# A tuned fp32 early-fusion layer on one core: scores and two second-layer passes of each expert-loop iteration issued earlier

## The reference

```python
z = jnp.einsum('nd,sdr->nsr', xf, P)              # 8 groups of R=16
scores = jnp.einsum('nsr,smr->nsm', z, C)         # 64 experts per group
topv, topi = jax.lax.top_k(scores, K)             # K = 4
w = jax.nn.softmax(topv, axis=-1)
h = jax.nn.gelu(jnp.einsum('nsr,nskrh->nskh', z, W1g) + b1g)   # first layer, 32 hidden
yl = jnp.einsum('nskh,nskhr->nskr', h, W2g) + b2g              # second layer
comb = jnp.einsum('nskr,nsk->nsr', yl, w)
out = jax.nn.gelu(comb @ G1 + g1b) @ G2 + g2b
```

## Time and profile before

| | us |
|---|---|
| median of 3 executions (954.18 to 957.66) | 955.19 |
| the profiled execution, its own time | 961.78 |
| its span, first to last instruction | 960.0 |
| PE busy / ACT busy / DVE busy / POOL busy in the span | 882.4 / 592.4 / 669.0 / 477.4 |
| mean granted TensorE clock, share of full speed | 0.965 |

### The profile page before, as it was taken

How to read it: one execution, slowest core, us unless ns; L and a number is a source line. 1 busy time by engine, 2 the same in 40 slices (tenths; PEclk the granted TensorE clock), 3 DMA queues, 4 the chain that set the end, 5 groups by cost and what they waited for, 6 DMA issues and landing times.

```text
span 960.0 us, 16073 instructions
## 1 busy us (share of the span) xinstructions
PE 882.4 (92%) x5394; PEld 397.4 (41%) x5394; DVE 669.0 (70%) x1670; ACT 592.4 (62%) x869; POOL 477.4 (50%) x446
## 2 busy tenths in 40 slices
PE   2599999999999977798989999999899989999997
PEld 1257777767877765322222222222222222222222
DVE  4355555566677468587778787788878877877774
ACT  0221211125322344599988897889988898988784
POOL 0043434233254435476766565656666665665453
PEclk8699999999999987799999998999999999999999
DMA  9500001000000166676879787878787978798772
GB/s 263 195 1 1 1 1 71 1 2 1 2 1 6 23 99 109 190 211 225 237 239 255 229 256 215 251 232 251 239 253 232 256 230 267 238 255 284 246 256 99
DMA packets 89053, 154.14 MB, mean 161 GB/s; under 512 B 30100, under 2 KB 55957, under 8 KB 88322
## 3 DMA queue, kind: packets, MB, share of 16 engines
q1 hardware_dynamic: 87998, 149.86, 51.5%
q10 hardware_dynamic: 972, 3.24, 2.4%
HBM read 138.81 MB, written 15.83 MB: 161 GB/s over the span
## 4 chain that ended last, share of the span: by engine, by line
PE 71%; DVE 11%; ACT 10%; issue 4%; DMA 1%; SPq 1%; POOL 1%; ACTq 1%; DVEq 0%; POOLq 0%
PE ps L764 15%; PE ps L701 14%; PE ps L424 8%; PE ps L432 5%; PE ps L740 4%; PE ps L491 4%; PE ps L483 3%; DVE ring L1495 3%; DVE ring L1498 3%; PE ps L500 3%; PE ps L541 2%; PE ps L461 2%; PE ps L513 2%; ACT ring L1058 2%; ACT L943 1%
## 5 line engine op out<-in xcount | busy, mean ns | idle before, releaser
L1697 POOL TENSOR_TENSOR ring<-ring,wbc 128x512 f32<-128x512 f32 x192 | 244.6, 1279 | 157.6 <-ACT ring L1065 149.0
L1495 DVE TENSOR_TENSOR ring<-ps,ring 128x1024 f32<-128x1024 f32 x192 | 234.7, 1223 | 95.8 <-ACT ring L1058 50.1
L701 PE MATMUL ps<-zst,w1st 99*128 99x512 bf16 x768 | 219.4, 390 | 22.5 <-ACT ring L1058 15.0
L764 PE MATMUL ps<-ring,w2cur 128*32 128x512 f32 x1536 | 205.8, 609 | 0.0
L1058 ACT ACTIVATE ring<-ps 128x1024 f32<-128x1024 f32 x192 | 197.3, 1027 | 6.3 <-PE ps L701 6.1
L1552 POOL TENSOR_TENSOR t<-t 128x768 f32<-128x768 f32 x48 | 87.4, 1832 | 206.2 <-DVE t L1186 206.2
L1067 ACT ACTIVATE ps<-ps 128x512 f32<-128x512 f32 x192 | 114.3, 595 | 46.2 <-PE ps L701 46.1
L1498 DVE TENSOR_TENSOR ring<-ps,wbc 128x512 f32<-128x512 f32 x192 | 131.1, 683 | 1.2 <-DMA wbc<-w_rows 1.2
L701 PEld LDWEIGHTS ps<-zst,w1st 99*128 99x128 bf16 x768 | 60.1, 98 | 162.6 <-issue 37.4
L1184 DVE TENSOR_TENSOR t<-ps,rope 128x768 f32<-128x768 f32 x48 | 45.8, 953 | 110.6 <-PE ps L432 74.4
L1065 ACT ACTIVATE ring<-ps 128x512 f32<-128x512 f32 x192 | 115.7, 603 | 0.4 <-PE ps L701 0.4
(11 more groups left out here) (165 smaller groups left out, 1147.3 us busy)
## 6 DMA issues: line engine op xcount, KB each, us to landing
wbc<-w_rows SPq DMA_DIRECT2D x192, 512.0 KB, 5.2
w2cur<-in_w SPq DMA_DIRECT2D x48, 256.0 KB, 4.9
w_parts<-wp SPq DMA_DIRECT2D x72, 64.0 KB, 3.2
zst<-z_parts SPq DMA_DIRECT2D x72, 64.0 KB, 5.2
w1st<-w_parts ACTq DMA_DIRECT2D x12, 256.0 KB
wst<-w_parts SPq DMA_DIRECT2D x24, 128.0 KB, 4.6
z_parts<-zp SPq DMA_DIRECT2D x6, 384.0 KB, 5.5
wst<-w_parts SPq DMA_DIRECT2D x24, 96.0 KB, 4.8
```

The costliest lines, as they stand in the source:

```text
L701: return pe.matmul(bank(to), w1st[0:99, 4 * a + j, col:col + P], zst[0:99, (i // 2) % 2, j, :], start=True, stop=True)
L764: mm = pe.matmul(bank(YBANK, 0, 512, 32 * j, 32 * j + 32), w2cur[:, n, j, :], ring[:, (4 * g + j) % RING, :], start=False, stop=(n == 7 an ...
L1495: dve.tensor_tensor(v, ps[:, WBANK * 512:WBANK * 512 + 1024], v, ALU.mult).then_inc(s["duo_done"], 1)
L1697: pool.tensor_tensor(ring[:, slot, :], ring[:, slot, :], wbc[:, g % 4, 1, :], ALU.mult).then_inc(s["tri_done"], 1)
```

## The change

The scores of tile `i + 6` are issued at the end of group n = 3, behind `two_first` of the next group, and not at the start of n = 4; between the two places PE had nothing else. In iterations 5, 9, 13 and 17 (`finals`) they keep their old place. Directly behind, PE issues `second(8i+2)` and `second(8i+3)`, which used to stand inside the bodies of n = 4 and n = 5; those bodies now have none. On ACT `copy_scores` moves, except in the `finals` iterations, from the end of n = 4 to the end of n = 3, directly behind `exps`. For iterations 1 to 3 the wait for `z_e` moves with the scores.

```diff
+        def finals(i):
+
+            return i % 4 == 1 and i > 1
...
-                    if n == 4:
-                        pe.wait_ge(s["z_e"], i + 3)
-                if n == 4 and tile + 1 < TILES:
+                if n == 4 and tile + 1 < TILES and finals(i):
                     pe.wait_ge(s["wT_done"], tile)
-                    if i > 4:
-                        pe.wait_ge(s["fin_h"], 2 * ((i - 1) // 4))
+                    pe.wait_ge(s["fin_h"], 2 * ((i - 1) // 4))
                     scores(tile + 1, PBANK)
                 if g + 1 < GROUPS:
                     duo_firsts(g + 1)
                     tri_first(g + 1)
-                if g >= 2 and g % 16 != 2:
+                if g >= 2 and g % 16 != 2 and not (tile < TILES and n in (4, 5)):
                     second(g - 2)
...
                 if g % 16 == 2:
                     second(g - 2)
+                if n == 3 and tile < TILES:
+                    if tile + 1 < TILES and not finals(i):
+                        pe.wait_ge(s["wT_done"], tile)
+                        if i in (1, 2, 3):
+                            pe.wait_ge(s["z_e"], i + 3)
+                        scores(tile + 1, PBANK)
+                    second(g - 1)
+                    second(g)
...
-                if n == 4 and tile + 1 < TILES:
+                if n == (4 if finals(i) else 3) and tile + 1 < TILES:
                     copy_scores(tile + 1, PBANK)
```

## The result

The changed kernel takes **990.06 us** in the median of four executions (981.35 to 998.12), beside 956.42 for the kernel before. Two of the four (996.34 and 998.12 us, with the lowest mean granted clocks) lie more than 1.5% above the fastest and are left out of the ratio, which is **1.0254 (95% interval 1.0218 to 1.0289)**. A later measurement with six executions gives 985.16 us (979.76 to 995.65) and 1.0257 (1.0225 to 1.0288).

The account below looks back on a forecast made before the run. Two chains were taken to bound the kernel: PE's row of work, and ACT from the exponentials to n = 7. Terms 1.99 + 0.78 + 12.74 - 0.2 = +15.3 us on the 955.2 median gave 970.5 us, range 961 to 982.

Parts of the forecast that it names:

- PE has time to spare in the odd iterations only, none in the even ones: PE busy 22.15 of 22.25 us in iteration 10, 19.73 of 22.20 in 11, with a 1.83 us gap before n = 4.
- The passes are ready and cost no wait: Behind the scores, the two moved second passes find products and weights ready; two take 2.0 us.
- The table load does not run ahead of the waiting copy: On in-order ACT, load and GELU follow the waiting copy; first GELU of n = 4 at scores' start + 2.97 us.
- Net +1.82 us in an ordinary even iteration: Iteration 10: first GELU of n = 4 3.04 us later, less 1.22 back by n = 6, passed fully into the time.
- -0.03 us in an odd one: Odd iterations without finals: first GELU of n = 4 1.19 us later, less 1.22 back; taken as 0.
- Finals 0: Iterations 5, 9, 13 and 17: net 0 to -0.4 us each, taken as 0 because PE waits for DVE anyway.
- The sum: Iterations 0 and 2 +1.99 and +0.78, seven even ones +12.74, iteration 18 -0.2: +15.3 us.
- Rival 3: TensorE's clock falls where PE is thin between scores and n = 7: two to four more falls, 977 to 983 us; chance 0.15.
- the mechanism: ACT's wait for the scores in the even iterations passes through into the time: 963 to 976 us, chance 0.67.
- Rivals 1 and 2: 1: PE's filled gaps are gained, 942.6 us, chance 0.08; 2: ACT's delay is absorbed, 953 to 958 us, chance 0.10.

Follow-up runs that it names:

- third experiment: The change in the odd iterations only (finals included), even ones exactly as in the kernel before: 958.76 us, ratio 1.0012 against the kernel before.
- kernel with fillers: The changed kernel plus five filler matmuls, results unused, in PE's idle time per iteration with moved scores: 972.11 us, ratio 1.0140 against the kernel before.
- second experiment: The changed kernel with the second passes back in n = 4 and 5, scores and copy as changed: 1014.74 us, ratio 1.0593 against the kernel before.

## Why the prediction was right in its cause and short in size

- **PE has time to spare in the odd iterations only, none in the even ones.** Right. It decides the case, and the third experiment shows it.
- **The passes are ready and cost no wait.** Right: 1.92 us for both, directly behind the scores.
- **The table load does not run ahead of the waiting copy; the first GELU starts at the scores' start + 2.97 us.** Right: 668.11 - 665.15 = 2.96. No drain showed beside the load either (copy's end to load 0.02, load to GELU 1.29), so the row was rightly taken over the 1380 ns that the Trainium skill gives for a drain (ScalarE: Activation LUTs, What ACT_TABLE_LOAD costs).
- **Net +1.82 us in an ordinary even iteration.** Right: +1.80. Its parts hold too: in iteration 10 the delay is 3.02 us at the first GELU of n = 4, 2.54 at that of n = 5, where the copy is gone, and 1.79 at the copy of the gates, whose transposes are in time. Iteration 14 gains only +1.27 (24.05 with fillers, 22.78 before), because it had been longer before; the prediction counted it like the others.
- **-0.03 us in an odd one.** Right in 7, 11 and 15, and for the reason given: the delay is 1.18 us at the first GELU of n = 4 and gone by the copy of the gates. In 1 and 3 it is +0.6 and +0.5. In iteration 1 the delay is gone by n = 7 too and comes up again behind the first GELU of the next iteration, where PE waits 0.30 us for DVE; this part was not tested.
- **Finals 0.** Mis-sized: -0.49 each, just outside the 0 to -0.4 that were given. I had let DVE absorb it, because PE waited for DVE two groups into the next iteration. It absorbed nothing; why not was not tested (DVE's products wait for the same GELUs and may simply have moved with them).
- **The sum.** Without falls: +1.3, +0.6, +1.5 and +0.5 in iterations 0 to 3, where +2.0, 0, +0.8 and 0 were forecast, about +12.1 in the even ones from 4 to 16 (forecast +12.7), -2.0 in the finals (forecast 0): +14. The kernel with fillers measures +13.3. Forecast +15.3, so the total came nearer than its terms.
- **Rival 3 at 0.15.** This is where the forecast fell short: the term for falls of the clock was left out of the sum, and it came to about ten us. I counted falls as a rival beside the forecast, though they come on top of it. And I had the numbers for it: one fall in the five odd iterations with the gap, and the same thin stretch of PE in all fourteen iterations after the change. My own working gave two to four more falls and 977 to 983 us, and the 979.5 us that the ratio makes lie there, outside the 963 to 976 of the mechanism that I gave 0.67; the profiles have four and six falls. The likeliest case was the sum of both, about 980, and the range should have gone to 990. That the ratio still falls inside the range is owed to the room that rival 3 had been given in it. It also took the number of falls from one profiled execution.
- **Rivals 1 and 2.** Wrong, for the reason given against them: filling PE's gap brings no GELU forward. But with the wait out of the way an odd iteration is 0.75 us shorter, 0.55 of it by the moved passes, so the gap of 1.83 us was not worth nothing either.

## What to carry to other kernels

Before an operation is moved into another engine's pause, ask who is late there in every variant of the loop body: the gap that one iteration shows may be the other's backlog. An operation with a wait must not stand ahead of a table load on an in-order engine unless its input is ready by then; moving the producer one step earlier cures it as well as moving the consumer back. And where a change thins out PE's work, price the clock as a term of the sum, not as a rival.

## What the runs showed of the hardware

In this kernel TensorE's clock fell to its 1.2 GHz level behind stretches in which PE idled in part: in iteration 7 of the kernel before after 1.83 us of idle time, in iteration 6 of the changed one after 1.16, 0.38 and 0.21 us, and in twelve of the fourteen iterations where PE stood for up to 3.01 us (second experiment, 0.81 to 0.94 over the iteration). With five useless matmuls in the idle time none fell from iteration 5 on. But the idle times alone do not tell when: iteration 10 of the changed kernel has the same ones as its iteration 6 and kept its clock, in both profiles. Some falls come back at the same place (6, 11 and 14 in both profiles), others do not (2 in one, 1, 3 and 4 in the other); why was not tested. A fall costs 1.2 to 1.5 us in iterations 1 to 3 and 2.5 from 4 on in the changed kernel, 3.1 in iteration 7 of the kernel before and 4.4 in odd iterations of the second experiment.

On ScalarE a table load took 1.28 us in every order that was tried. Behind a copy that waited 2.44 us for PE it began 0.02 us after the copy and not earlier, and the GELU behind it began 1.29 us after the load.
